# Opening the second wide attention inside the feed-forward block of the chosen tokens

## The reference, cut to what matters

```python
x = x + tanh(g_xattn[0]) * L0_xattn(layernorm(x), ctx)   # 16 heads of 32
x = x + tanh(g_ffn[0])   * L0_ffn(layernorm(x))          # 256 chosen rows of each batch: attention, then silu(h W1) * (h W2) W3
x = x + tanh(g_xattn[1]) * L1_xattn(layernorm(x), ctx)   # 16 heads of 64
x = x + tanh(g_ffn[1])   * L1_ffn(layernorm(x))          # 8-bit rows, ternary weights, a convolution
# L1_xattn: q = x @ Wq; softmax(q k / 8) v; out @ Wo + bo
```

## Time and profile before

| | us |
|---|---|
| median of 3 runs | 1846.93 |
| the profiled execution | 1849.65 |
| its span | 1848.0 |
| PE busy | 1572.4 (85%) |
| DVE busy | 1272.5 (69%) |
| ACT busy | 890.3 (48%) |
| POOL busy | 580.8 (31%) |
| mean granted TensorE clock | 0.932 of full speed |

### The profile page before, as it was taken

How to read it: one execution, slowest core, us unless ns; L and a number is a source line. 1 busy time by engine, 2 the same in 40 slices (tenths; PEclk the granted TensorE clock), 3 DMA queues, 4 the chain that set the end, 5 groups by cost and what they waited for, 6 DMA issues and landing times. The chain is left out here.

```text
span 1848.0 us, 25690 instructions
## 1 busy us (share of the span) xinstructions
PE 1572.4 (85%) x9526; PEld 956.2 (52%) x9559; DVE 1272.5 (69%) x2051; ACT 890.3 (48%) x1438; POOL 580.8 (31%) x558
## 2 busy tenths in 40 slices
PE   4788889888778889747999999999998868888886
PEld 3444444443346657533666665666664534444443
DVE  3367779788542546434577766777666599999995
ACT  3355555455444436325333343333432377777763
POOL 3114332233310002113121120211201297777770
PEclk9899999999878889868999999999999899999999
DMA  4112112212623424340001211012010330222111
GB/s 157 45 47 92 65 50 71 90 69 92 243 85 102 173 95 142 119 166 22 24 24 58 68 36 59 23 58 72 9 58 29 121 120 29 70 76 77 52 46 46
DMA packets 73155, 142.34 MB, mean 77 GB/s; under 512 B 8289, under 2 KB 17653, under 8 KB 72778
## 3 DMA queue, kind: packets, MB, share of 16 engines
q1 hardware_dynamic: 72074, 137.55, 21.6%
q0 software_dynamic: 960, 3.15, 0.5%
HBM read 97.67 MB, written 43.01 MB: 76 GB/s over the span
## 5 line engine op out<-in xcount | busy, mean ns | idle before, releaser
L2705 POOL TENSOR_TENSOR E_y<-E_y,E_centre 128x1024 f32<-128x1024 f32 x64 | 151.2, 2362 | 9.8 <-ACT E_y L2734 7.6
L1322 ACT ACTIVATE D_oT<-D_OB 128x512 fp32r<-128x512 f32 x64 | 38.3, 598 | 226.6 <-DVE D_OB L1663 226.6
L2620 PE MATMUL E_OP<-E_w2q,E_yb 128*128 128x512 bf16 x509 | 124.8, 401 | 25.0 <-issue 18.9
L2697 POOL TENSOR_SCALAR E_centre<-E_hs,E_cw,E_cb 128x512 f32<-128x512 f32 x64 | 108.6, 1696 | 57.5 <-DVE E_hs L2787 57.2
L2610 PE MATMUL E_HP<-E_xT,E_w1q 128*128 128x512 bf16 x482 | 120.1, 388 | 2.5 <-ACT E_xT L2711 0.4
L1628 DVE TENSOR_TENSOR D_q_low<-D_PJ,D_q_high 128x512 fp32r<-128x512 f32 x62 | 42.9, 692 | 114.8 <-ACT D_q_high L1298 114.8
L1400 PE MATMUL D_PJ<-D_xT_high,D_wq_high 128*128 128x512 f32 x248 | 105.5, 425 | 9.2 <-DVE D_wq_low L1635 7.2
L2796 DVE SCALAR_TENSOR_TENSOR E_y<-E_hs,E_cw,E_y 128x512 f32<-128x512 f32 x128 | 106.9, 874 | 0.0
L2620 PEld LDWEIGHTS E_OP<-E_w2q,E_yb 128*128 128x128 bf16 x512 | 51.4, 102 | 91.9 <-issue 42.7
L1400 PE MATMUL D_PJ<-D_xT_high,D_wq_low 128*128 128x512 f32 x248 | 98.8, 399 | 0.0
L1400 PE MATMUL D_PJ<-D_xT_low,D_wq_high 128*128 128x512 f32 x248 | 98.6, 398 | 0.0
(11 more groups left out here) (402 smaller groups left out, 4152.5 us busy)
## 6 DMA issues: line engine op xcount, KB each, us to landing
A_x<-in_x SPq DMA_DIRECT2D x8, 1024.0 KB, 5.4
A_res<-in_x SPq DMA_DIRECT2D x8, 1024.0 KB, 5.4
xn_d<-A_xn SPq DMA_DIRECT2D x8, 1024.0 KB, 4.7
x_d<-A_res SPq DMA_DIRECT2D x8, 1024.0 KB, 5.5
W_raw<-in_w1T SPq DMA_DIRECT2D x16, 512.0 KB, 3.6
W_raw<-in_w2T SPq DMA_DIRECT2D x16, 512.0 KB, 3.7
D_x<-x_d SPq DMA_DIRECT2D x8, 1024.0 KB, 5.5
D_res<-x_d SPq DMA_DIRECT2D x8, 1024.0 KB, 6.2
```

The costliest lines, as they stand in the source:

```text
L2620: mm = pe.matmul(OP[:, :], yb[:, k, c * P:(c + 1) * P], w2q[:, k, :], start=k == 0, stop=k == MC - 1)
L2697: pool.tensor_scalar(U[i % 2][:, 0, :], hs[i % NBUF][:, 0, 1:TILE + 1], cw[:, 2 * p, 1:2], cb[:, 2 * p:2 * p + 1], ALU.mult, ALU.add).then ...
L2705: pool.tensor_tensor(y, y, U[i % 2][:, :, :], ALU.add).then_inc(t0, 1)
```

## The change

A new class, `FirstTile`, does the opening of D_ inside the last block of C_. Its tensors (Wq high and low, the turned tile high and low; 48 KB a partition) lie at the start of C_'s memory, over the second feed-forward weight and others that are dead once `made2` has reached 11; D_ finds them at the same address. To make room `w1`, `w2`, `w3_high` and `gated_low` are placed elsewhere in C_. The rows are loaded into `xs`, the chosen rows, dead by then.

- SP: at piece 10 it waits for the last up product and loads Wq; at piece 14 it waits for the first two scatters (they have a semaphore of their own now) and loads the first tile in four DMAs, one a chunk.
- ACT: Wq's high part after pieces 10 and 11; the turned chunks' high parts at its end.
- DVE: Wq's low part after pieces 10 and 11, `add_base` 0 and 1 ahead of pieces 14 and 15, then statistics and normalising chunk by chunk, the low parts of the first two chunks, `add_base` 2 and 3, the low parts of the last two.
- POOL: the inverse roots between scatters 1 and 2.
- PE: chunks 0 and 1 are turned before m = 9 and m = 10 of the second pair, chunks 2 and 3 behind it, each in a bank of its own (0 to 3); then the four query products, into banks 0 to 3. D_ has its banks in another order so that it reads them there.
- D_ begins with the take-out of the query products. Its SP starts with the second tile, then the bias and Wo in three DMAs (3, 3 and 2 slices), each with a semaphore. ACT and POOL split Wo in these three parts, at the ends of j = 0, 1 and 2 of the first step. DVE normalises the second tile right behind its statistics, ahead of the first step.

```diff
+class FirstTile:
+    def load_weights(self, sp):
+        sp.dma_start(self.wq[:, :, :], self.io[self.L["wq"]].rearrange("(k p) n -> p k n", p=P)).then_inc(self.w_in, 16)
+    def load_rows(self, sp):
+        for c in range(SUB):
+            sp.dma_start(self.rows[:, c, :], tile_view(self.io[self.L["x"]])[0, 0, :, c]).then_inc(self.x_in[c], 16)
...
+    def weigh_rows(self, dve, c):
+        dve.wait_ge(self.x_in[c], 16)
+        dve.bn_stats(self.stats[:, c, :], self.rows[:, c, :]).then_inc(self.st, 1)
+        dve.wait_ge(self.st, c + 1)
+        dve.bn_aggr(self.mv[:, c, :], self.stats[:, c, :]).then_inc(self.folded, 1)
+        dve.wait_ge(self.folded, c + 1)
+        dve.tensor_scalar(self.var[:, c:c + 1], self.mv[:, c, 1:2], LN_EPS, None, ALU.add).then_inc(self.var_ok, 1)
...
+    def turn(self, pe, c, ident):
+        pe.wait_ge(self.normed, c + 1)
+        for k in range(KD):
+            mm = pe.transpose(self.chunk_bank(c)[:, k, :], self.rows[:, c, k * P:(k + 1) * P], ident)
+        mm.then_inc(self.turned, 1)
...
+    def project(self, pe):
+        pe.wait_ge(self.w_lo, KD)
+        pe.wait_ge(self.x_lo, SUB)
+        for m in range(self.ready):
+            for k in range(KD):
+                for w, x in ((self.wqh, self.xh), (self.wql, self.xh), (self.wqh, self.xl)):
+                    pe.matmul(self.banks[m], w[:, k, m * P:(m + 1) * P], x[:, k, :],
...
@@ wide_attention @@
-            load_x(0, 0)
-            sp.dma_start(wq, rows(io[L["wq"]])).then_inc(w_in, 16)
...
-            sp.wait_ge(x_tr, SUB)
             load_x(0, 1)
-            sp.dma_start(wo[:, :, :], rows(io[L["wo"]])).then_inc(b_in, 16)
             sp.dma_start(bo[:, :], io[L["bo"]].rearrange("(a n) -> a n", a=1).to_broadcast([P, D])).then_inc(b_in, 16)
+            for j, ks in enumerate(WO_CUTS):
+                cut = slice(ks.start, ks.stop)
+                sp.dma_start(wo[:, cut, :], rows(io[L["wo"]])[:, cut, :]).then_inc(wo_in[j], 16)
...
             act.preload_act_table_set("natural_log_exp_and_others")
-            for c in range(SUB):
-                keep_xT(0, c)
-            act.wait_ge(w_in, 32 if L["bias"] else 16)
-            for k in range(KD):
-                act.activation(wqh[:, k, :], wq[:, k, :], ACT.Copy).then_inc(wq_hi, 1)
             for m in range(RING):
-                keep_q(0, m, first_banks[m % 3])
+                keep_q(0, m, first_banks[m])
...
                     guess_rz(n, j)
-                    if isinstance(lap, int) and n == 0 and j < 2:
-                        split_wo(j)
...
                     if QG > 1:
                         high_o(n, par, j, 1)
+                    if isinstance(lap, int) and n == 0 and j < len(WO_CUTS):
+                        split_wo(j)
...
-            for c in range(SUB):
-                transpose_x(0, c)
-            pe.wait_ge(wq_hi, KD)
-            pe.wait_ge(wq_lo, KD)
-            for m in range(RING):
-                project_q(0, m, first_banks[m % 3], 3)
             scores_for_max(0, 0, 0)
...
             maxima(0)
             ln_stats(1, 0, 1)
+            ln_apply(1)
...
-                    if j == 0 and not last:
+                    if j == 0 and not first and not last:
                         ln_apply(n + 1)
@@ choice_layer, last block @@
                 for i in range(WP):
+                    if i == MF - 1:
+                        sp.wait_ge(made2, MF)
+                        first.load_weights(sp)
+                    if i == WP - 2:
+                        sp.wait_ge(put[0], 16 * HALVES)
+                        first.load_rows(sp)
                     store_piece(sp, io, wb, i)
...
+                        if pair and m >= MF - 2:
+                            first.turn(pe, m - (MF - 2), cst["ident"][:, :])
...
+                for c in (2, 3):
+                    first.turn(pe, c, cst["ident"][:, :])
+                first.project(pe)
...
-                for i in range(MF - 1, WP):
+                for i in range(MF - 1, MF + 1):
                     round_piece(act, wb, i)
+                first.high_w(act)
+                for i in range(MF + 1, WP):
+                    round_piece(act, wb, i)
+                for c in range(SUB):
+                    first.high_x(act, c)
...
+                    if n == HALVES:
+                        for c in range(SUB):
+                            first.scale(pool, c)
...
-                for i in range(MF - 1, WP):
+                for i in range(MF - 1, MF + 1):
                     cap_piece(dve, wb, i)
-                for n in range(NS):
+                first.low_w(dve)
+                for i in range(MF + 1, WP - 2):
+                    cap_piece(dve, wb, i)
+                for n in range(HALVES):
                     add_base(n, summed, made3)
+                for i in range(WP - 2, WP):
+                    cap_piece(dve, wb, i)
+                for c in range(SUB):
+                    first.weigh_rows(dve, c)
+                    if c:
+                        first.normalise(dve, c - 1)
+                first.normalise(dve, SUB - 1)
+                first.low_x(dve, 0)
+                first.low_x(dve, 1)
+                for n in range(HALVES, NS):
+                    add_base(n, summed, made3)
+                first.low_x(dve, 2)
+                first.low_x(dve, 3)
```

More of the change, by code:

```diff
@@ L1259, in step @@
                         low_x(n + 1, 1)
-                    if first and j < 2:
-                        low_wo(j)
                     if j == 0:
@@ L1268, in step @@
                         low_x(n + 1, 3)
+                    if first and j < len(WO_CUTS):
+                        low_wo(j)
                     if j == GROUPS - 1 and not is_last(lap, par, 2):
@@ L1932, in choice_layer @@
         idx, xs, base = (chosen[n] for n in ("idx", "xs", "base"))
+        first_space = ExitStack()
+        first = FirstTile(nc, sem, io, LAYER1, first_space, xs, cst["minus_half"][:, 0:1], [])
+        first_space.close()
         with ExitStack() as over:
-            gl = place(over, "gated_low", [P, MF, SEL], F32R)
+            w2 = place(over, "w2", [P, KD, DFF])
+        with ExitStack() as over:
+            w2l = place(over, "w2_low", [P, KD, DFF], F32R)
         with ExitStack() as over:
@@ L1972, in choice_layer @@
         oT = sb("oT", [P, QT, SEL])
+        with ExitStack() as over:
+            w1 = place(over, "w1", [P, KD, DFF])
+        with ExitStack() as over:
+            w1l = place(over, "w1_low", [P, KD, DFF], F32R)
+        with ExitStack() as over:
+            wh = place(over, "wqkv_high", [P, KD, 3 * D], F32R)
+            hh, hl = (place(over, "hT_" + n, [P, KD, SEL], F32R) for n in ("high", "low"))
+        w12, w12l = (w1, w2), (w1l, w2l)
+        w3h, gl = sb("w3_high", [P, MF, D], F32R), sb("gated_low", [P, MF, SEL], F32R)
         ss, rs = sb("ss", [P, NS]), sb("rs", [P, NS])
         PS = ctx.enter_context(nc.psum_tensor("C_PS", [P, 8, TILE], F32))
+        first.banks.extend(PS[:, i, :] for i in range(first.ready))
         w3_in = sem("w3_in")
@@ L2108, in scores @@
                     need(pe, s_ex, HG * n)
-                    for cols, h, asked in ((slice(0, CAP), first, both), (slice(CAP, W), second, second)):
+                    for cols, h, asked in ((slice(0, CAP), half0, both), (slice(CAP, W), half1, half1)):
                         for kp, qp, start in ((qkh, qkh, True), (qkl, qkh, False), (qkh, qkl, False)):
```

184 lines of the change are left out of this document (99 added, 85 removed).

## The result

The changed kernel takes 1817.49 us, median of 4 runs (1815.2 to 1819.27). The kernel before, run beside it, takes 1848.09 us (4 runs, 1844.24 to 1852.53). The ratio is 0.9826, with a 95% interval of 0.9804 to 0.9847: between 28 and 36 us less, where 33 were forecast. The median is 3.5 us above the forecast of 1814. The profiled execution took 1819.27 us with a span of 1817.5, at a mean granted clock of 0.938.

The account below looks back on a forecast made before the run. TensorE is busy 85% of the span, so gains lie where it stands still. The opening's 24 us plus the first step's 9 make 33, from 1849.65 to 1816.7, or 1814 for the median of the runs; range 1809 to 1825.

Parts of the forecast that it names:

- The opening: Between last down product and first scores for maxima: moving D_'s opening into C_ saves 24 us.
- Wq is split in the idle time ahead of piece 12: C_'s way down: ACT (3.9 us) and DVE (4.9 us) split Wq while waiting for that piece, so it is free.
- Rows loaded at 767.2: C_'s last block: SP may load the first tile's rows 3.6 us after DVE's first two base additions end at 763.6.
- DVE's chain up to the low parts: After the first chunk lands: statistics and normalising take 6.8 us, the last inverse root on POOL 1.05, ending at 778.4.
- PE waits 1.8 us and the clock stays full: Behind the turned chunks: PE waits for DVE until 782.5, then makes 48 query products at full pace in 11.3 us.
- Table load and take-outs up to the scores: Start of D_: the 1.28 us table load, two high parts and one low part put 3.2 us on the path.
- The first step: D_'s first step: moving Wo's split and the second tile's normalising saves 9 us, bounds 2 and 12.
- take-out, low part, divide, high and low: Chain in j = 0 without split and normalising: ends at 843.5, where PE went on at 850.51, saving 7 us.
- The stall moves: First step: PE waits as long on exponentials held by Wo's split, gaining 0 to 2 us; 1823 us, chance 0.15.
- The rows come late: Opening in C_: late chunks and slower DVE links start the projection 6 to 8 us later; 1824 us, chance 0.12.
- PE stays at half clock: From the change of stage through the first step: clock stays at 0.50, kernel slower at 1859 us; chance 0.02.
- It does not do what it says: Opening of D_: nobody was waiting for it, so the time stays at 1847 us; chance 0.02.

Follow-up runs that it names:

- e9: Changed kernel with the 512 KB load of weight piece 15 issued behind the four row loads; 1822.43 us (one run).
- e8: Changed kernel with the 48 query products back at the start of D_, the rest of the opening staying in C_; 1815.69 us, ratio 0.9803.
- e3: Changed kernel with Wo again split in halves mid-group, the second tile's normalising left ahead of the first step; 1816.47 us, ratio 0.9825.
- e4: Changed kernel with the second tile normalised in j = 0 again, Wo's split left at the ends of the groups; 1816.71 us, ratio 0.9807.
- e5: The changed kernel measured once more, without any edit; 1816.04 us, ratio 0.9811.
- e6: Changed kernel with DVE making all four low parts ahead of the last two base additions; 1814.22 us, ratio 0.9807.
- e10: Changed kernel with Wo's three cuts split one group earlier, the first ahead of the first step; 1814.77 us, ratio 0.98.
- e11: Changed kernel with the edits of e6, e7 and e10 together; 1808.83 us, ratio 0.9776.
- e2: Kernel before with only the first step's edits (Wo in three cuts, second tile normalised early), opening left in D_; 1843.33 us, ratio 0.9956.
- e7: Changed kernel with ACT's table of exponentials loaded at the end of C_'s block, not in D_; 1817.72 us, ratio 0.9823.
- e1: Changed kernel with its first step as before: Wo split in halves mid-group, second tile normalised in j = 0; 1826.58 us, ratio 0.9863.

## Why the prediction was right, step by step

**The opening: 24 us forecast, 23.5 measured.** The total is closer than its terms: up to 2 us too little and up to 2 us too much stand in it and cancel, which is luck. The steps in the order of time, counted from the mark (741.24 for the prediction's times, 744.57 for the trace after):
- Wq is split in the idle time ahead of piece 12: yes. DVE waits for pieces again at 763.18, and for the rows at 774.26, so that cover held.
- Rows loaded at 767.2 (+26.0): measured +27.05, and two misses are in that. The scatter took 4.7 us instead of the 2.7 that stand behind my "3.6 us later", a row from the second pair, where no piece was being loaded; e9 shows that the load was the cause. And PE's first pair was done 1.3 us earlier than I had it, DVE's two additions 1.0: 6 of the products ran at half pace at its start, where it had been 13. The two are linked. In e8 it is 13 again, the scatters fall further behind the load, and the rows are loaded at +26.32.
- First chunk after 3.4 us: 2.64 (771.62 to 774.26). DVE's chain up to the low parts 7.8 us: 6.4 (774.26 to 780.69). I had read "1.2 us each" off a row that held waits of its own. Together these took back more than the rows lost.
- Low parts and base additions 4.05 us: 3.9 (780.69 to 784.6), so products at +40.05, where I had 782.5 (+41.3).
- "PE waits 1.8 us and the clock stays full": this step failed. PE was through 2.2 us earlier than I had it: 1.3 from the first pair, and the turns, of which one inside the pair held it for 0.36 us (777.14 to 777.50) and two in a row for 1.04, where I had 0.60 each. DVE was only 1.2 us earlier. So the pause was 2.78 us, and 8 of 48 products came at half pace: 12.78 us instead of 11.3, at a granted clock of 0.87 instead of 1.00.
- Change of stage 1.3 us: 1.7 (797.40 to 799.09). Table load and take-outs up to the scores 3.2 us: 3.35. The scores at half clock, 2.2 us: 1.97.

From the first product to the first scores it took 17.8 us, 2.0 more than forecast; the part ahead was 1.2 less.

**The first step: 9 us forecast, 9.5 measured.** Here too the terms are further off than the sum. The forecast has 7 us for j = 0 and 3 - 1 = 2 for the wait at the turns and the third cut, which lie in j = 1 and 2. Measured are 5.4 for j = 0, 1.9 and 1.1 for j = 1 and 2, and 1.1 for j = 3, for which it had nothing. The stall of 9.01 us became 3.20, not 2. The step "take-out, low part, divide, high and low" was a us longer in j = 0, because DVE's two small operations on the maxima took 0.74 and 1.24 us. POOL adds the residual rows beside them (818.31, 2.54 us), work that in the kernel before stood behind Wo's low parts; in e3, where it stands there again, the same two take 0.20 and 0.24. I had costed the residual rows by who waits for them, and hadn't asked what POOL's work does to DVE beside it. The thirteen profiles settle it, since the additions don't always fall there. POOL's two additions end at 819.60 and 820.85 here, DVE's two operations 0.06 and 0.09 us behind them; the same 0.06 to 0.14 us are found in e4, e5, e6, e9, e10 and e11, whatever the length that results. In e2 and e8 the additions are over before, in e7 they begin only during the second operation; there the two take 0.20 to 0.23 us, and PE's stall is 2.05, 2.05 and 2.07: the 2 us forecast. From e8:

```profile
818.58 0.20 DVE L1705 CAST D_m<-D_mx 128x16 bf16<-128x16 f32 x1
818.82 0.23 DVE L1707 TENSOR_TENSOR D_m<-D_mx,D_m 128x16 bf16<-128x16 f32 x1
822.98 1.07 PE L1503 MATMUL D_OB<-D_probs,D_V 128*32 128x512 f32 x8 [2.07 <-DVE D_oT L1724]
830.83 1.12 PE L1485 MATMUL D_SC<-D_k_high,D_q_high 64*128 64x128 f32 x16 [1.78 <-ACT D_probs L1409]
```

The step isn't shorter for it. The us that the stall loses comes back as the last row, a stall of 1.78 us on the exponentials of j = 1, which the changed kernel doesn't have; e8's first step is 74.56 us. "The exponentials of j = 1 stand behind the split": yes, 829.07 + 1.66 and then 830.63 without idle time. The forecast of -1 for the third cut was too gloomy. The cut makes the exponentials of j = 3 start late, but those of the next step start on time again, and j = 3 is a us shorter for it (16.97 us against 18.03; in e10, where the cuts stand one group earlier, the short group is j = 2).

**The rivals.** *The stall moves* (1823) was wrong in size: the stalls on exponentials are 1.56 and 0.67 us, and in e2 and e8, where there are three, 4.0 and 4.3 us together, where it needed 7 to 9. *The rows come late* (1824) had a true core, 1 us by a load that runs beside the scatter, and not the 6 to 8 us it needed. *PE stays at half clock* didn't happen: the clock is full again within the 48 products and over the first step's later part. *It does not do what it says* is out by e1 and e2.

**The table load and the shared port.** The load of the table took 1.28 us with nothing behind it (799.09 to 800.39 here, 767.37 in e7). The Trainium skill (ScalarE: Activation LUTs, What ACT_TABLE_LOAD costs) has about 2.66 us for a change of table, 1.38 of it a drain; this case's trace disagrees. DVE's normalising and its two small operations end 0.06 to 0.3 us after POOL's operation beside them, as told above, so that a short one takes up to 1.25 us. The Trainium skill (SBUF — State Buffer, Who interferes with whom) calls the port of DVE and POOL an exclusive lock, held for the whole instruction; the traces agree. Whether a DMA issued by POOL stands still while DVE holds the port stays open. In e9 the scatter landed in 2.74 us, as it did before, but DVE's two caps of piece 14 began (764.72) only after POOL's issuing instruction had ended (763.25 + 0.97). What cost the scatter 2 us was the load of 512 KB.

**The whole.** 33 us forecast between the marks, 33.0 measured: both mechanisms are as forecast, the agreement to 0.1 us is luck. Of its signs the pause (2.78 us) and the first step held, and PE's 5.05 us of idle time at the change of stage nearly; the clock of 1.00 over the products did not. The median is 3.5 us above the forecast. The four runs span 4 us and the mark stood 3.3 us later in the profiled one than before, so I put that down to the wander of the rest and not to a term of the sum; nothing here shows it.

## What to carry to other kernels

Where a stage begins with a long chain of small steps on other engines, look for the time to win in the chain ahead of the first matmul; moving the matmuls themselves gained nothing here (e8). When work is pushed out of a critical group, look at the pair of engines it ran on, as the price of one piece can hang on whether the other is still there (0.5 and 5.2 us alone, 10.0 together). Before a transfer is issued early, look at what else is being transferred while the operation that it waits for lands (4.7 us instead of 2.7 for the scatter), and put a small dependent operation ahead of a filler in each queue: exchanging two lines of DVE's order took 1.0 us off the path here.

## What the runs showed of the hardware that I had not expected

- **The clock after a short pause is not settled by its length.** After 2.78 to 3.14 us without work, 8, 14, 8, 0, 7, 8 and 13 products came at half pace (after, e1, e3, e4, e5, e7, e10). After 1.67 to 1.82 us it was 0, 0 and 8 (e9, e6, e11). e4 and e5 had the same pause of 3.14 us, with 0 and 7. Why isn't settled; one profile can't show what such a pause costs, between 0 and 3 us here.
- **A scatter of 256 KB beside a load of 512 KB** took 4.7 us from its issue in the changed kernel, 3.0 to 5.9 over the runs with that load, and 2.7 without it.
- **Some of DVE's operations end only when POOL's does.** Two operations of 128x16 in bf16 that take 0.20 and 0.24 us alone took 0.21 to 1.08 and 1.17 to 1.25 us beside POOL's additions of 1.3 us, and ended 0.06 to 0.14 us after them in all seven profiles in which POOL's addition was the first to begin. So it isn't a factor but the rest of POOL's instruction. DVE's normalising, 0.54 us for each of its operations alone, took 1.48 us for three of four in e1 in the same way. Not every operation does: the low part of a query product, read from PSUM, kept its 0.69 us beside POOL's low parts of Wo (843.57 in before, 823.05 in e1).
- **Thirteen products or six.** PE starts the way down out of 3.45 us of idle time in every profile. In before, e2 and e8 13 products then run at half pace, in all ten others 6. That is 1.3 us. The split between kernels suggests that it goes with the kernel rather than with the execution, but only the changed kernel was profiled twice, and what decides it isn't settled.
- **The same code ahead of the mark** took 737.6 to 744.6 us over 13 profiles. A difference of a few us between two spans says nothing here until both are cut at a common mark.
